# Attention weights of a graph layer formed from a PSUM-resident row, two heads at a time

## What is computed

```python
# layer 0: of each node, the features of its first 25 neighbours, their maximum, and a linear map
scores = jnp.where(A != 0, -arange(N), -inf); vals, idx = top_k(scores, 25)
agg = max over the 25 rows X[idx]             # a missing neighbour is left out; max(agg, 0) if degree <= 25
x = layernorm(X + relu(concat([X, agg]) @ W + b))
# layer 1: attention with 4 heads of 64 over the neighbours (adj is 0/1, so one edge type is met)
h = einsum('bnd,hde->bhne', x, W1)
w = leaky_relu(e_src[i] + e_dst[j], 0.01); w = where(adj[i, j] == 0, -1e9, w)
dst = softmax_j(w) @ h + bias
out = layernorm_per_head(relu(dst) + h) * gamma + beta
x = layernorm(x + out)
```

## Time and profile before

| | us |
|---|---|
| median of 3 runs | 5489.24 |
| lowest and highest | 5440.72, 5507.57 |
| span of the profiled execution | 5448.3 |

### The profile page before, as it was taken

How to read it: one execution, slowest core, us unless ns; L and a number is a source line. 1 busy time by engine, 2 the same in 40 slices (tenths; PEclk the granted TensorE clock), 3 DMA queues, 4 the chain that set the end, 5 groups by cost and what they waited for, 6 DMA issues and landing times.

```text
span 5448.3 us, 58256 instructions
## 1 busy us (share of the span) xinstructions
PE 3438.2 (63%) x11778; PEld 1438.1 (26%) x11778; DVE 4138.1 (76%) x11484; ACT 3111.4 (57%) x5570; POOL 3717.1 (68%) x3204
## 2 busy tenths in 40 slices
PE   1232467666666767666676666666666666666786
PEld 1121222222222222222222222222222222222222
DVE  4555578878787888878787878888878788787777
ACT  3333456666556666656655655656656666555565
POOL 4666777777777777777777777777777777677400
PEclk9555578777778777878777787787888778778798
DMA  3434344444444444444444444444444444444210
GB/s 113 130 119 136 119 138 128 146 132 146 125 129 133 135 144 135 132 143 129 134 133 133 145 125 127 139 130 146 136 144 131 128 139 131 137 131 133 85 39 27
DMA packets 282021, 692.71 MB, mean 127 GB/s; under 512 B 62849, under 2 KB 130178, under 8 KB 265346
## 3 DMA queue, kind: packets, MB, share of 16 engines
q0 software_dynamic: 153600, 419.64, 26.1%
q1 hardware_dynamic: 128130, 270.41, 15.6%
HBM read 639.21 MB, written 50.59 MB: 127 GB/s over the span
## 4 chain that ended last, share of the span: by engine, by line
POOL 36%; issue 25%; DVE 22%; PE 8%; DMA 4%; ACT 3%; another core or an unknown queue 1%; POOLq 0%; DVEq 0%; SPq 0%; ACTq 0%
POOL rows L498 36%; PE acc L1231 5%; DVE uv L819 5%; DVE rmax L836 4%; DMA rows<-in_x_dram,idx 4%; DVE top L715 2%; DVE key_b L717 1%; PE pB L1199 1%; DVE agg L845 1%; DVE sth L892 1%; ACT uv L565 1%; DVE key_a L717 1%; DVE mvh L898 1%; ACT stage L525 0%
## 5 line engine op out<-in xcount | busy, mean ns | idle before, releaser
L498 POOL DMA_INDIRECT rows<-in_x_dram,idx x3200 | 3716.9, 1162 | 1404.5 <-issue 997.0
L1231 PE MATMUL acc<-uv,hs 128*65 128x512 f32 x4096 | 2301.4, 712 | 707.2 <-DVE uv L819 448.3
L565 ACT ACTIVATE uv<-rb,qj 128x512 f32 (+1 forms) x2048 | 1330.4, 712 | 169.6 <-PE acc L1231 137.6
L819 DVE SCALAR_TENSOR_TENSOR uv<-uv,maskT 128x1024 f32<-128x1024 f32 x1024 | 1239.9, 1221 | 183.6 <-ACT uv L565 148.4
L1231 PEld LDWEIGHTS acc<-uv,hs 128*65 128x65 f32 x4096 | 602.6, 160 | 1992.7 <-issue 1403.4
L836 DVE TENSOR_TENSOR rmax<-rmax,rows 128x1280 f32<-128x1280 f32 x384 | 572.5, 1491 | 600.4 <-DMA rows<-in_x_dram,idx 553.5
L628 ACT ACTIVATE xaT<-pA 128x512 f32<-128x512 f32 x128 | 76.4, 597 | 791.3 <-PE pA L1186 610.6
L542 ACT ACTIVATE stage<-pT 128x1024 bf16<-128x1024 f16 x256 | 260.6, 1018 | 288.8 <-remote 148.0
L1186 PE MATMUL pA<-id,xt 128*128 128x128 f32 x256 | 81.5, 419 | 469.4 <-DVE agg L846 334.2
L640 ACT ACTIVATE x1T<-pA 128x256 f32<-128x256 f32 x128 | 49.2, 384 | 570.8 <-PE pA L1209 394.5
L1199 PE MATMUL pB<-w_sb,xaT 128*128 128x256 f32 x1024 | 348.0, 499 | 18.4 <-ACT xaT L628 8.6
(11 more groups left out here) (113 smaller groups left out, 3755.5 us busy)
## 6 DMA issues: line engine op xcount, KB each, us to landing
adj_sb<-in_adj_dram SPq DMA_DIRECT2D x128, 1024.0 KB
rows<-in_x_dram,idx POOLq DMA_INDIRECT x3200
xh_dram<-xh SPq DMA_DIRECT2D x128, 256.0 KB
rb<-r_dram SPq DMA_DIRECT2D x32, 1024.0 KB
xr<-xh_dram SPq DMA_DIRECT2D x64, 512.0 KB
xt<-in_x_dram SPq DMA_DIRECT2D x128, 128.0 KB
out_dram<-xr SPq DMA_DIRECT2D x32, 512.0 KB
r_dram<-er SPq DMA_DIRECT2D x128, 2.0 KB
```

What stands on the lines that cost most here:

```text
L498: nc.gpsimd.indirect_dma_start(rows[:, c, r * C:(r + 1) * C], None, x_rows, bass.IndirectOffsetOnAxis(ap=idx[p][:, k:k + 1], axis=0)).then ...
L565: last = nc.scalar.activation(uv[k][:, i, :], rb[:, bass.ds(qa % 2, 1), h, :].rearrange("p a i -> p (a i)"), ACT.Copy, scale=q_j(h))
L819: nc.vector.scalar_tensor_tensor(uv[k][:], uv[k][:], 1.0, m, ALU.max, ALU.mult).then_inc(s_u, 1)
L1231: last = nc.tensor.matmul(acc[h][0:HW, :], hs[:, (1 - quad.par) * JT + jt, h, :], uv[k][:, i, :], start=(jt == 0), stop=(jt == JT - 1))
```

## The change

ScalarE's `scaled` goes, with `rb`, `r_dram` and their DMAs and semaphores. `er` (r of 2 graphs) stays in SBUF with the four heads on four partitions. In each quad, at u = 0 for heads 0 and 1 and at u = 2 for heads 2 and 3, TensorE spreads r over all partitions by a matmul with `headsel` into the two PSUM banks `rq` (`broadcast`). VectorE forms the weights of a half unit (one head, 512 columns) as max(rq, 1/q_j) * mask; 1/q_j is a per-partition scalar (`qinv`), and d_j q_j is folded into the features (`dj`). Heads go in pairs: steps 0 and 1 do heads 0 and 1 for all j, steps 2 and 3 heads 2 and 3. Two `acc` banks remain, so numerators, back and divide run twice per quad, for pair 0 at u = 2 and for pair 1 at u = 0. A step's 16 halves all stand in the search: places 3, 4, 5, 6, 9, 13, 14, 18, 21, 22, 23, 25, 28, 30, 31 and 33. Separately, `aggregate` makes its maximum over five candidates from three two-operand maxima in place of one reduce.

```diff
-            def scaled(quad, u, n, ahead=0):
...
-                for i in range(2):
-                    h = 2 * hh + i
-                    last = nc.scalar.activation(uv[k][:, i, :], rb[:, bass.ds(qa % 2, 1), h, :].rearrange("p a i -> p (a i)"),
-                                                ACT.Copy, scale=q_j(h))
...
-                nc.scalar.activation(dj[:], p_ed, ACT.Exp, scale=LEAK).then_inc(s_ed, 1)
-                nc.scalar.activation(qj[:, bass.ds(t, 1), :], p_ed.unsqueeze(1), ACT.Exp, scale=1.0 - LEAK)
+                nc.scalar.activation(dj[:], p_ed, ACT.Exp).then_inc(s_ed, 1)
+                nc.scalar.activation(qinv[:, bass.ds(t, 1), :], p_ed.unsqueeze(1), ACT.Exp, scale=LEAK - 1.0)
...
-                nc.vector.scalar_tensor_tensor(uv[k][:], uv[k][:], 1.0, m, ALU.max, ALU.mult).then_inc(s_u, 1)
+            def masked(quad, u, n, i):
+
+                pair, jt, k = u // 2, HJ * (u % 2) + n, n % UVB
+                h = PAIR * pair + i
+
+                if i == 0:
+                    for v in quad.reach(lambda q: UNITS * (q - BQ) + US * u + n - UVB + 1):
+                        dve.wait_ge(s_pe, v)
+                    if n == 0:
+
+                        dve.wait_ge(s_proj, projected(quad, u))
+                        if u % 2 == 0:
+                            for v in quad.reach(lambda q: 2 * (q - BQ) + pair + 1):
+                                dve.wait_ge(s_rq, v)
+                m = maskT[:, bass.ds((quad.q - BQ) % RING * JT + jt, 1), :].rearrange("p a i -> p (a i)")
+                inv = qinv[:, (1 - quad.par) * JT + jt, h:h + 1]
+                stt = nc.vector.scalar_tensor_tensor(uv[k][:, i, :], rq[i][:], inv, m, ALU.max, ALU.mult)
...
-                ch.then(nc.vector.tensor_reduce(agg[:], rmax[:].rearrange("p (r f) -> p f r", f=C), axis=AX.X, op=ALU.max))
+                ch.then(nc.vector.tensor_tensor(rmax[:, 0:2 * C], rmax[:, 0:2 * C], rmax[:, 2 * C:4 * C], ALU.max))
+                ch.then(nc.vector.tensor_tensor(rmax[:, C:2 * C], rmax[:, C:2 * C], rmax[:, 4 * C:5 * C], ALU.max))
+                ch.then(nc.vector.tensor_tensor(agg[:], rmax[:, 0:C], rmax[:, C:2 * C], ALU.max))
...
-            UNIT_AT = (2, 4, 6, 14, 22, 31)
+            UNIT_AT = (3, 4, 5, 6, 9, 13, 14, 18, 21, 22, 23, 25, 28, 30, 31, 33)
...
+            def broadcast(quad, pair):
+
+
+                for v in quad.reach(lambda q: UNITS * (q - BQ) + pair * UNITS // 2):
+                    pe.wait_ge(s_u, v)
+                    pe.sem_inc(s_go["pe"], 1)
+                block = (quad.q - BQ) % BQ * IB
+                for i in range(PAIR):
+                    last = nc.tensor.matmul(rq[i][:], headsel[:, PAIR * pair + i, :],
+                                            er[0:HEADS, bass.ds((1 - quad.par) * N + block, IB)], start=True, stop=True)
+                last.then_inc(s_rq, 1)
...
             def step(quad, u):
+                if quad.on(u, QT * BQ):
+                    pe.wait_ge(s_proj, projected(quad, u))
+                    if u % 2 == 0:
+                        broadcast(quad, u // 2)
                 if u == 0 and quad.on(u, FIN):
-                    back(quad)
+                    back(quad, 1)
+                if u == 2 and quad.on(u, QT * BQ):
+                    back(quad, 0)
```

## The result

| | kernel before | changed kernel |
|---|---|---|
| median, us | 5472.44 (5440.72 to 5507.57) | 6559.06 (6554.29 to 6581.56) |
| ratio, 95% interval | 1 | 1.1988 (1.1916 to 1.206) |
| profiled span, us | 5448 | 6579.7 |

What follows compares the result with a forecast made beforehand. Gather rate and VectorE's work behind search place 26 were taken as the bound. A quad 3.4 us shorter gave 95 us over 28 quads, plus 5 at the end: factor 0.982, 5390 us, range 5270 to 5560.

Steps and rivals of the forecast that it cites:

- What bounds the kernel: Loop tile: GpSimd's gather rate and VectorE's work behind search place 26 set the time, 38.1 us undisturbed, 40.2 measured.
- At the start nothing of this stands on the path: Start of the kernel: the forecast counted no gain or loss there.
- The gathers relieved: GpSimd: masks with a PSUM first operand disturb gathers less, 2.7 us a tile regained, 0.11 a gather.
- ScalarE: ScalarE: 2,048 copies, 1,330 us, go; worth almost nothing, as it is 57% busy and VectorE waited for it only 148 us.
- The masked halves: VectorE: sixteen 512-column instructions of 0.683 us replace eight; +2.7 us behind chunk 1, +1.1 behind chunk 3.
- The aggregate: VectorE: a 2.32 us reduce becomes three maxima of 0.68, 0.41 and 0.41 us; aggregate ready 0.75 us earlier.
- The new wait: VectorE at place 3, u=0 and u=2: halves wait for TensorE's broadcast, starting at agg + 6.5 us; wait 4 to 5 us.
- D: Rival: TensorE runs broadcast, back and product0 at a slow rate, each pair's start 4.0 us later; 5614 us, chance 0.08.
- The sum: Quad of four tiles: 150.2 us plus 7.2 of disturbances, 157.4, 3.4 less than before; 39.3 us a tile.
- C: Rival: gathers are not relieved, as U8 mask and f32 write alone disturb them; 163.9 us a quad, 5572 us, chance 0.15.
- B: Rival: gathers also rid of late landings, half a unit at its low bound, quad 153 us; 5272 us, chance 0.2.

Runs made afterwards that it cites:

- e12: Changed kernel plus a waited GpSimd memset behind gathers 8, 10 and 12 of every tile; 5438.55 us, 1.016 times the kernel before.
- e15: Changed kernel with waited memsets behind gathers 8, 10 and 12, and the masks' per-row scalar 1/q replaced by constant 1.0; 5635.52 us, ratio 1.03.
- e1: Changed kernel with the masked halves' first operand from a constant SBUF tile instead of PSUM; 5752.19 us against 5415.72, ratio 1.06.
- e17: Changed kernel with waited memsets behind gathers 8, 10 and 12 beside attention only, repeated on chip 9; 5347.10 us, ratio 0.999.
- e4: Changed kernel with back's eight transposes replaced by two plain products of 260 columns; 6252.48 us against 5415.72, ratio 1.15.
- e14: Changed kernel with waited memsets behind gathers 8, 10 and 12 at every u, beside attention only, on chip 8; 5676.53 us, ratio 1.044.
- e8: Changed kernel plus a waited GpSimd memset behind every third gather; 5682.13 us against 5398.85, ratio 1.052.
- e5: Changed kernel plus a one-column GpSimd memset, not waited for, behind each gather; 6706.73 us against 5454.26, ratio 1.228.
- e6: Changed kernel plus a one-column GpSimd memset, not waited for, behind every second gather; 6657.77 us against 5454.26, ratio 1.219.
- e16: Changed kernel with waited memsets behind gathers 8, 10 and 12 of every tile, repeated on chip 9; 5440.52 us, ratio 1.017.
- e2: Changed kernel plus a waited GpSimd memset behind every gather; 6952.97 us against 5415.72, ratio 1.28.

## Why the prediction was wrong, point by point

**What bounds the kernel.** "What stands behind place 26 of the search, and how fast GpSimd gathers, set the time." It held for the kernel before. The step from it that failed is that each gather's gain is the tile's gain (20 x 0.11 = 2.2 us earlier at chunk 3), with product0 and VectorE's chain in time at any rate of the gathers: their lateness was put at nothing. The gain was read off single rows (0.95 beside the divide), where one quick gather among longer ones harms nobody. Nothing in the trace of before shows a whole tile beside attention at that rate. Its tiles ahead of attention do run at 1.33 us, and there VectorE's search lost 5.0 us a tile; "At the start nothing of this stands on the path" passed over them. The runs show in its place: between an interval of 1.49 and one of 1.31 us another limit comes in, and completions of TensorE and VectorE come late: that of product0 at u=0 3.5 us after the tile's last gather, at u=2 2.8 us before its end. A tile was then not the 39.3 us of the forecast but 24 x 1.31 + 18.7 = 50.1, the 18.7 being the time from the last gather's start to the next tile's first, 4.3 before.

**The gathers relieved.** Forecast 1.07 in the loop, measured 1.004; 1.08 with the pauses (e12), where VectorE runs at its full pace, against 1.18 before. So the gain of 0.11 a gather was sized right, and it was this gain that did the harm.

**ScalarE.** Right: the removed scaling passes gave nothing that can be seen, and no wait for ScalarE is left in front of the halves.

**The masked halves.** Forecast 0.683, measured 0.742. The step that failed is the comparison: both rows on the line had a constant as their scalar, the new form has one per row. With a constant it is 0.682 (e15), on the line. Neither PSUM nor SBUF matters (0.742 both, e1). The 0.065 us more for a PSUM source, an estimate that the prediction takes from the Trainium skill (VectorE: DVE Perf Modes, the TRN2 errata), looks like the difference, but e1 shows that it is not what is paid here. Sixteen halves cost 0.9 us more a tile by this.

**The aggregate.** 0.692, 0.425 and 0.425 us for the three maxima against 0.68, 0.41 and 0.41; right.

**The new wait.** Forecast 4 to 5 us at place 3 of u=0 and u=2 and none at odd u. Measured: 288 us of idle time in front of the 64 first halves at even u, 4.5 each (3.90 in the rows above), and 4 in all at odd u. Right. A broadcast's four passes took under 3 us in 47 of 64 cases (2.0 in most) and 3.8 in the others (the granted clock of the loop is 0.75, 0.78 before), so D's condition was met in part, but it was not what decided.

**The sum.** 39.3 us a tile were forecast. Where nothing is late, the new order measures 39.6 (e12) and 39.7 (e17), with some 1.8 us of pauses and 0.9 us of dearer halves in it; that the two agree to 0.3 us is in part luck. The wait for rows at chunk 1 of odd u (5 us or more) was not seen (0.8 and 1.1 in e12, 1.8 in the changed kernel); the waits for rows are 601 us in all in e12, 4.7 a tile, spread over four chunks. So the arithmetic of the tile stood nearly, and lacked a term of 10 us.

**The rivals.** Two slower ones were among them (C and D, up to 5614 us), with other mechanisms and a ninth of the effect. None had a gather's speed as the harm; B, which gave faster gathers the most credit, was the farthest off.

**What stays open.** What that limit is. The runs say that it is shared by GpSimd's gathers and the completions of TensorE and VectorE (not ScalarE's), that it depends on the gathers' interval, on what runs beside them (at 1.33 us without attention product0 is in time, and the search is not), perhaps on the number of TensorE's instructions (e4), and on the chip or moment (e14 against e17), and that it goes when the gathers pause. The rival that weighs most is untested: that it is the recording of the trace. Every execution here was recorded (each has a profiled span and clock), and updates are missing from the traces above all where completions are late. So it is open whether the changed kernel is slower at all when it runs unrecorded. The Trainium skill (SBUF — State Buffer, "SBUF: two separate sides") has only the port pair of VectorE and GpSimd as a place of contention on the engines' side, and TensorE waiting on nobody. By that rule nothing at SBUF's ports could hold TensorE up. In these traces its results are 15 to 20 us late beside gathers; whether the rule fails or the shared part lies elsewhere, no run here shows. What the changed kernel itself does on the quicker chip was not tried.

No version here beats the kernel before: the best, e17, equals it (0.999, 0.998 to 1.001).

## What to carry to other kernels

When an engine that streams DMA work looks like the bound, making it faster may cost more than it gives: look at the other engines' completions beside its densest stretch, in every phase of the trace (here the one ahead of attention had it), and keep a rival that says so. A row whose end is modelled does not tell when its result is usable; compare it with the start of the instruction that waits for it. If a consumer starts many us after its producer's row with the label "remote" or "issue", try a short pause in the stream before anything else: eight waits a tile on the streaming engine were worth 14% here (e8 against e5 and e6, one chip). And count the semaphore updates in the trace: if many are missing, time the kernel without the recording before a rule is drawn from it.

## What the runs showed of the hardware that was not expected

- Beside gathers that start every 1.31 us, product0's semaphore came 15 to 20 us behind its last row, near or past the end of the tile's gathers (changed kernel); at 1.49 us it came at once in all but 3 of 112 tiles (before), and at 1.53 us and above, on one chip at 1.47 too, it was never over 2.4 us behind (e8 to e12, e16, e17).
- VectorE's statistics of 0.23 us, with no wait between them, came 0.7 or 1.4 us apart in that state; 0.13 otherwise. In quads with gathers alone, every 1.33 us, VectorE's search lost 5.0 us a tile in the same way (before), and none on another chip (e17).
- Where completions were late, the trace lacked semaphore updates: 26,830 held by the changed kernel's, 73,887 by e12's.
- A scalar per row in place of a constant makes the masks' instruction of 512 columns take 0.742 instead of 0.682 us (e15); its first operand in PSUM instead of SBUF changes nothing (0.742 both, e1).
- A memset of 0.12 us that is not waited for fits wholly into the 0.30 us between two gathers; waited for, it costs 0.6 (e12) to 0.7 us (e2).
